# New stages between the layers of a three-layer graph attention kernel: residual products in the last edge stage, a bias in the table rows, self loop and share in one pass

## The chip, the cores and the metric

The kernel runs on one core of one Trainium2 chip. The metric is device microseconds (us) of one execution, lower is better. Three executions of the kernel before took 6745.49, 6760.7 and 6763.31 us, median 6760.7 us. In what follows PE is TensorE, DVE is VectorE, ACT is ScalarE, POOL is GpSimd and SP is SyncE.

## What is computed

There are 12500 nodes with 256 values each and 200000 directed edges, sorted by target. Two blocks follow each other, each with a residual and a layer norm. The first holds two graph attention layers of 4 heads, the second a linear map and one layer of 8 heads:

```python
def gat_conv(x, src, dst, W, att_src, att_dst, bias, n_nodes):      # layers 0 and 1, self loops appended to the edges
    h = (x @ W).reshape(n_nodes, Hh, Cc)
    alpha = leaky_relu((h * att_src).sum(-1)[src] + (h * att_dst).sum(-1)[dst])
    e = jnp.exp(alpha - segment_max(alpha, dst)[dst])
    w = e / jnp.clip(segment_sum(e, dst), 1e-16)[dst]
    return segment_sum(w[:, :, None] * h[src], dst).reshape(n_nodes, Hh * Cc) + bias

x = layernorm(x + gat_conv(relu(gat_conv(x, ...layer 0)), ...layer 1))
h = x @ W_lin + b_lin                                                # layer 2, without self loops, 8 heads of 32
x = layernorm(x + h + leaky_relu(gat(h @ W_gat, src, dst) + gat_bias, 0.01))
```

## The kernel before, in words

**Stages.** The nodes are 98 blocks of 128 (12500 padded to 12544), the edges 1568 tiles of 128 in 98 windows of 16 tiles, of which the last 5 tiles of the last window hold no edge. The program goes through `node_phase(None, 0)`, which builds the index tables, folds the weights and computes the table rows of layer 0, and then for each layer L through `edge_phase(L)`, `clear_semaphores()` and `node_phase(L, L + 1)` (`final_phase()` behind layer 2). Each of them is a block of its own: no engine enters the next before all have left the last. A table row holds a node's 256 products and its source terms for the heads, all in float32. I call the node stages before layer 1 and layer 2 the first and the second stage between layers.

**Edge stage.** For each window, POOL issues 16 indirect transfers (L1212), one for each tile, that gather the rows of the tile's source nodes into one of three row buffers. SP loads the window's index columns `loaded` (L1224), one-hot rows and masks. ACT turns the one-hot rows of the next window into a lookup matrix (L1248, L1251), copies the source terms out of the rows (L1262), clears the PSUM sums (L1242) and takes exponentials. PE turns the source terms (L1344), loads addresses into registers (L1194), turns the row sums (L1352), looks up the target terms (L1301), and then runs the products of the window before (L1287 for three extra tiles, L1294 for the 16 tiles) that add messages to the blocks' sums. DVE scans for the segment maximum (L1503), multiplies the rows by the weights (L1414), builds the one-hot matrices (L1406) and adds the finished sums to `acc`, which stays in SBUF for all 98 blocks with the sum of weights and the maximum of each head.

**Stages between layers.** DVE first works out two factors for every node and head at once, 392 columns (L689 to L711): the share by which the summed messages are divided, and the factor `own` of the self loop. SP loads the node's own table row from DRAM, one block at a time into three buffers (`n_looprow`), and before layer 2 also the input x (`n_resrow`). POOL multiplies the row by `own` (L657), and before layer 2 adds layer 1's bias and x (L665, twice). DVE adds this term to the shared-out sum (L772). The share itself is applied by DVE (L764) in the first of the two stages and by ACT (L549) in the second. Before layer 2 the layer norm follows on DVE (L781, L785, L789, L800; the root on ACT). PE turns the block (L891), ACT copies it back to SBUF (L565, L568), PE makes the products for the next table (L905, and L908 for the bias in three bfloat16 parts) and, before layer 2, the products with `w_lin` for the residual (L902, L903), to which DVE adds the node row (L807). ACT copies the table row (L576) and the target terms (L580, L581) and stores both from its own queue (L585, L589). At the end DVE splits the target terms of all blocks into three bfloat16 parts (L834, L836). The order on each engine is the order in which the loops emit, a fixed lag for each step behind the block's number.

**What clears the counters.** Between an edge stage and the node stage behind it POOL clears 71 semaphores one by one (L344 to L348), while the other engines stand at the block's border.

## Time and profile before

| | |
|---|---|
| three executions | 6745.49, 6760.7, 6763.31 us |
| the profiled execution | 6753.64 us, span 6751.8 us |
| granted TensorE clock, mean | 0.763 of full speed |
| busy share of the span | PE 72%, PE weight load 54%, DVE 75%, ACT 37%, POOL 72% |
| DMA | 995.73 MB, mean 147 GB/s over the span |
| gathers | 4704 instructions on L1212, 4488.4 us busy |

The span is that of one profiled execution. A busy share is a mean over stages that have different limits, so it does not say what bounds the kernel. Rows of the timeline show, in this order, the start in us from the span's start, the duration, the engine, the line, the operation, what is written and read, the shape and type, the count, and in square brackets how long the engine stood idle ahead of it and what ended that. "issue" means that nothing the profile shows was waited for.

### The profile page before, as it was taken

How to read it: one execution, taken by the hardware profiler on the slowest of the kernel's cores; microseconds unless marked ns; L12 is line 12 of the kernel's file. 1: busy time of each engine (PE TensorE's matmuls, PEld its weight loads, DVE VectorE, ACT ScalarE, POOL GpSimd, SP SyncE). 2: the span in 40 equal slices, each digit the busy share in tenths (PEclk: the TensorE clock that was granted, in tenths of full speed). 3: DMA queues.
4: the chain of work that ended last, by engine and by line, in shares of the span. 5: the costliest groups of instructions: out<-in, count | busy, mean ns of one | idle time of the engine just before them, and what ended most of it. 6: DMA issues, size and time to landing. Idle time of an engine off the chain costs nothing. (4 is left out here: it accounts for less than half of the span.)

```text
span 6751.8 us, 104146 instructions
## 1 busy us (share of the span) xinstructions
PE 4889.6 (72%) x21580; PEld 3649.8 (54%) x21581; DVE 5043.8 (75%) x15127; ACT 2499.9 (37%) x4364; POOL 4853.2 (72%) x5234
## 2 busy tenths in 40 slices
PE   6777777777776677777777777595777777777776
PEld 4555555555554555555555555474555555555553
DVE  5777777777777777777777777686777777777778
ACT  3333333333332633333333333393333333333335
POOL 2777777777774577777777777596777777777764
PEclk8777777777777877777777777797777777777777
DMA  8444444444443644454544544374555555555544
GB/s 273 141 140 143 140 140 144 140 140 144 140 141 95 176 144 143 141 145 141 145 141 141 145 141 145 102 232 144 145 149 145 147 148 145 149 145 145 149 132 153
DMA packets 476056, 995.73 MB, mean 147 GB/s; under 512 B 143982, under 2 KB 283556, under 8 KB 475522
## 3 DMA queue, kind: packets, MB, share of 16 engines
q0 software_dynamic: 226928, 635.50, 34.3%
q1 hardware_dynamic: 192448, 305.57, 14.2%
q10 hardware_dynamic: 56402, 51.96, 2.3%
q14 instruction: 227, 1.86, 0.1%
q8 instruction: 51, 0.84, 0.0%
HBM read 921.41 MB, written 71.22 MB: 147 GB/s over the span
## 5 line engine op out<-in xcount | busy, mean ns | idle before, releaser
L1212 POOL DMA_INDIRECT e_rows<-table,e_loaded x4704 | 4488.4, 954 | 1524.4 <-issue 1378.5
L1294 PE MATMUL e_p_mm<-e_rows,e_onehot 128*128 128x264 f32 x9408 | 2421.5, 414 | 0.0
L1294 PEld LDWEIGHTS e_p_mm<-e_rows,e_onehot 128*128 128x128 f32 x9408 | 1880.9, 206 | 348.8 <-issue 0.2
L1414 DVE TENSOR_TENSOR e_rows<-e_rows,e_p_e 128x1024 f32<-128x1024 f32 x1176 | 1418.7, 1206 | 0.0
L1406 DVE TENSOR_TENSOR e_onehot<-e_col,e_p_iota 128x512 f32<-128x512 f32 (+1 forms) x1470 | 951.0, 647 | 295.9 <-issue 293.9
L1503 DVE TENSOR_TENSOR_SCAN e_fwd<-e_mask,e_p_one 64x128 f32<-64x128 bf16 (+1 forms) x294 | 122.0, 415 | 1150.0 <-PE e_p_one L1344 1148.4
L1287 PE MATMUL e_p_mm<-e_xmsg,e_onehot 128*128 128x264 f32 x1764 | 875.4, 668 | 32.9 <-ACT e_p_mm L1242 17.7
L1270 ACT ACTIVATE e_rows<-e_gap 128x64 f32<-128x64 f32 (+1 forms) x294 | 80.5, 274 | 1969.9 <-DVE e_gap L1572 1969.9
L1301 PE MATMUL e_p_one<-ad_parts,e_onehotT 128*128 x5586 | 681.0, 192 | 119.8 <-issue 118.5
L1352 PE MATMUL e_p_small<-ident,e_fwd 64*1 64x64 f32 (+1 forms) x294 | 86.9, 295 | 864.3 <-issue 853.1
L1301 PEld LDWEIGHTS e_p_one<-ad_parts,e_onehotT 128*128 128x128 bf16 x5586 | 552.4, 106 | 291.5 <-issue 185.4
L1248 ACT ACTIVATE e_onehotT<-e_onehotT,minus_pidx 128x2432 bf16<-128x2432 bf16 x294 | 681.4, 2318 | 34.2 <-DMA e_pass<-pass_rows 33.9
L1251 ACT ACTIVATE e_onehotT<-e_onehotT,one_col 128x2432 bf16<-128x2432 bf16 x294 | 682.7, 2322 | 9.6
L1287 PEld LDWEIGHTS e_p_mm<-e_xmsg,e_onehot 128*128 128x128 f32 x1764 | 542.9, 328 | 169.3 <-issue 26.7
L1344 PE MATMUL e_p_one<-ident,e_srcc 128*64 128x128 f32 (+1 forms) x294 | 90.8, 309 | 644.1 <-ACT e_srcc L1262 643.8
L1352 PEld LDWEIGHTS e_p_small<-ident,e_fwd 64*1 64x1 f32 (+1 forms) x294 | 22.7, 77 | 918.5 <-issue 918.5
L1344 PEld LDWEIGHTS e_p_one<-ident,e_srcc 128*64 128x64 f32 (+1 forms) x294 | 36.8, 125 | 755.8 <-issue 755.8
L1392 DVE TENSOR_TENSOR acc<-acc,e_p_mm 128x264 f32 x1176 | 416.1, 412 | 28.8 <-PE e_p_mm L1294 28.8
L1262 ACT COPY e_srcc<-e_rows 128x64 f32<-128x64 f32 (+1 forms) x294 | 100.4, 342 | 800.1 <-DMA e_rows<-table,e_loaded 800.1
L1468 DVE TENSOR_TENSOR e_xmsg<-e_rows,e_p_e 128x256 f32 x882 | 358.7, 412 | 0.0
L1242 ACT COPY e_p_mm<-iota_d 128x1056 f32<-128x1056 f32 x294 | 303.2, 1031 | 29.9 <-DVEq L1455 29.9
L1275 ACT ACTIVATE e_factor<-e_p_small 128x4 f32<-128x4 f32 (+1 forms) x294 | 51.5, 175 | 618.0 <-PE e_p_small L1373 618.0
(238 smaller groups left out, 5626.5 us busy)
## 6 DMA issues: line engine op xcount, KB each, us to landing
e_onehotT<-rel_rows SPq DMA_DIRECT2D x294, 608.0 KB
e_rows<-table,e_loaded POOLq DMA_INDIRECT x4704
n_looprow<-table SPq DMA_DIRECT2D x196, 128.0 KB, 2.6
table<-n_row ACTq DMA_DIRECT2D x98, 132.0 KB, 1.9
table<-n_rows_out SPq DMA_DIRECT2D x14, 910.0 KB, 10.3
table<-n_row ACTq DMA_DIRECT2D x98, 130.0 KB, 3.0
n_inputs<-in_x_turned SPq DMA_DIRECT2D x14, 896.0 KB, 11.0
e_mask<-mask_rows SPq DMA_DIRECT2D x196, 64.0 KB
```

The lines of the kernel that those rows point to most:

```text
L1212: pool.indirect_dma_start(rows[k][:, g, 0:TW], None, table[L], bass.IndirectOffsetOnAxis(ap=idx[k][:, g:g + 1], axis=0)).then_inc(s_gat[k] ...
L1242: nc.scalar.copy(p_mm[:].rearrange("p (r n) -> p r n", n=BANK)[:, :, 0:MW], zero_col.unsqueeze(2).to_broadcast([P, REGIONS, MW])).then_inc ...
L1248: nc.scalar.activation(onehotT[k][:], onehotT[k][:], ACT.Square, bias=minus_pidx[:, 0:1]).then_inc(st["square"], 1)
L1251: nc.scalar.activation(onehotT[k][:], onehotT[k][:], ACT.Relu, bias=one_col[:, 0:1], scale=-1.0).then_inc(st["onehotT"], 1)
L1287: nc.tensor.matmul(p_mm[:, r:r + MW], onehot[:, G + e, :], xmsg[:, e, :], start=False, stop=True, skip_group_check=True)
L1294: ins = nc.tensor.matmul(p_mm[:, bass.ds(region, MW)], onehot[:, g, :], rows[k][:, g, :], start=False, stop=True, skip_group_check=True)
L1301: return nc.tensor.matmul(p_look[:, column], onehotT[k][:, slot * P:(slot + 1) * P], ad_parts[:, bass.ds(ad, 3 * H)], start=False, stop=Tr ...
L1344: nc.tensor.transpose(p_src[0:HG, 0:P], srcc[:].rearrange("p h g -> p (h g)"), ident[:]).then_inc(st["srcT"], 1)
L1392: last = nc.vector.tensor_tensor(sums, sums, p_mm[:, r * BANK:r * BANK + MW], ALU.add)
L1406: return nc.vector.tensor_tensor(onehot[:, slot:slot + n, :], col[k][:, column:column + n].unsqueeze(2).to_broadcast([P, n, P]), nodes.uns ...
L1414: return nc.vector.tensor_tensor(feats, feats, p_e[:, g4, :].unsqueeze(3).to_broadcast([P, 4, H, C]), ALU.mult)
L1468: nc.vector.tensor_tensor(xmsg[:, e, 0:D].rearrange("p (h c) -> p h c", h=H), feats, weight, ALU.mult)
```

## The change

The two node stages between layers become a function of their own, `between_phase`.

- **Residual.** The product of the normalised block with `w_lin`, its bias and the node row itself leave the second stage between layers. That stage stores the turned blocks to DRAM (`turned_dram`, two blocks to a transfer). In layer 2's edge stage each window takes one block: SP loads it (128 KB), PE multiplies it with `w_lin` plus the identity (L1379) and adds the bias from three bfloat16 parts (L1380), ACT copies the sum to SBUF (`summed`), SP stores it.
- **Bias of layer 1.** DVE adds it to the rows of layer 1's table in the first stage between layers, as it copies them out of PSUM (`biased_row`, L836). POOL's addition of the bias in the second stage goes. Since a node's weights sum to one, the sum is the same.
- **Self loop and share.** DVE computes `acc * share + term` with four instructions of 128x64 (L807), one for each head, in place of one pass for the share and one for the addition.
- **Factors.** `share` and `own` are worked out for the first 14 blocks, and for the other 84 in five pieces between the steps of the stream.
- **Normalisation** goes from DVE to ACT. Roots, reciprocals and shifts are taken over up to 7 blocks at once.
- **Transfers.** Own rows and x are loaded two blocks at a time, 8 blocks ahead. Table rows are stored by SP, 7 blocks (910 KB) at a time.
- **Borders.** `clear_semaphores` clears two ranges. The first three loads of `loaded` are issued at the end of the node stage. In every edge stage the last window has 11 tiles, not 16.

```diff
@@ tables of numbers
+LAST_TILES = -(-N_EDGES // P) - (WINDOWS - 1) * G
...
@@ clear_semaphores
-    for x in [*per_layer, *s.values(), *s_node, *s_loop, *s_res, *s_row, *s_out, *s_rst]:
-        pool.sem_clear(x)
+    for group in (per_layer, [*s.values(), *s_node, *s_loop, *s_res, *s_row, *s_out, *s_rst]):
+        first, last = group[0].num, group[-1].num
+        assert [x.num for x in group] == list(range(first, last + 1))
+        pool.sem_clear(range(first, last + 1))
...
@@ new: issued by SyncE at the end of each node stage
+    def first_columns(q):
+        for w in range(BUFS):
+            q.dma_start(loaded[w][:], col_dram[:, w * COL_W:(w + 1) * COL_W]).then_inc(s_idx[w], 16)
...
@@ between_phase(before) in place of node_phase(0, 1) and node_phase(1, 2)
+    N_PAIRS, N_TERM, N_VALUE, N_NODE, N_XT, N_ROWS, N_PT, N_PM = 4, 6, 22 if normed else 8, 6, 4, 2 if normed else 3, 3, 4
+    def load(j):
+        if j >= N_PAIRS:
+            sp.wait_ge(s["loop_term"], 2 * (j - N_PAIRS + 1))
+        pair = slice(2 * j * P, 2 * (j + 1) * P)
+        sp.dma_start(looprow[j % N_PAIRS][:], table[before][pair, 0:D].rearrange("(j p) n -> p j n", p=P)
+                     ).then_inc(s_loop[j % N_PAIRS], 16)
...
+    def store_turned(j):
+        sp.wait_ge(s["xT"], 2 * (j + 1))
+        sp.dma_start(turned_dram[2 * j:2 * (j + 1)].rearrange("j p e -> p j e"), xT[j % N_XT][:]
+                     ).then_inc(s_rst[j % N_XT], 16)
+    def store_rows(c):
+        sp.wait_ge(s["row"], (c + 1) * CHUNK)
+        sp.dma_start(table[after][c * CHUNK * P:(c + 1) * CHUNK * P, :].rearrange("(j p) n -> p j n", p=P),
+                     rows_out[c % N_ROWS][:, :, 0:D + HA]).then_inc(s_row[c % N_ROWS], 16)
...
@@ GpSimd, per block
-    ins = nc.gpsimd.tensor_tensor(heads(term, b, HB), heads(buf(looprow, b)[:], b, HB),
-                                  over(own3, b, HB), ALU.mult)
-    if normed:
-        for n, other in enumerate((bias_bc, buf(resrow, b))):
-            ins.then_inc(s["chain_p"], 1)
-            if n:
-                moved(pool, s_res, b)
-            pool.wait_ge(s["chain_p"], 2 * b + n + 1)
-            ins = nc.gpsimd.tensor_tensor(term, term, other[:], ALU.add)
-    ins.then_inc(s["loop_term"], 1)
+    if b == LEAD:
+        pool.wait_ge(s["prep"], 4)
+    ins = nc.gpsimd.tensor_tensor(out.rearrange("p (h c) -> p h c", h=HB), own_row,
+                                  both[:, 1, b, :].unsqueeze(2).to_broadcast([P, HB, C]), ALU.mult)
+    if normed:
+        ins.then_inc(s["part"], 1)
+        pool.wait_ge(s["part"], b + 1)
+        ins = nc.gpsimd.tensor_tensor(out, out, resrow[j % N_PAIRS][:, at, :], ALU.add)
+    ins.then_inc(s["loop_term"], 1)
...
@@ ScalarE
-    def share_out(b):
-        free(act, s["node"], b, value)
-        for h in range(HB):
-            c = slice(h * (D // HB), (h + 1) * (D // HB))
-            ins = nc.scalar.activation(buf(value, b)[:, c], acc3[:, b, c], ACT.Identity, scale=sh3[:, b, h:h + 1])
-        ins.then_inc(s["v1"], 1)
+    def normalise(b):
+        act.wait_ge(s["shift"], span_of[b] + 1)
+        free(act, s["turned"], b, N_NODE)
+        nc.scalar.activation(buf(node, b)[:], buf(value, b)[:], ACT.Identity, bias=shift[:, b:b + 1],
+                             scale=rinv[:, b:b + 1]).then_inc(s["node"], 1)
...
@@ VectorE
-    def value_share(b):
-        free(dve, s["node"] if normed else s["turned"], b, value)
-        num = acc[:, b * ACC_W:b * ACC_W + D]
-        nc.vector.tensor_tensor(heads(buf(value, b)[:], b, HB), heads(num, b, HB), over(sh3, b, HB), ALU.mult
-                                ).then_inc(s["v1"], 1)
-    def value_add(b):
-        v = buf(value, b)[:]
-        dve.wait_ge(s["v1"], b + 1)
-        if looped:
-            dve.wait_ge(s["loop_term"], b + 1)
-            nc.vector.tensor_tensor(v, v, buf(loopterm, b)[:], ALU.add).then_inc(s["value"], 1)
-    def normalise(b):
-        dve.wait_ge(s["rinv"], b + 1)
-        free(dve, s["turned"], b, node)
-        free(dve, s["resid"], b, node)
-        nc.vector.tensor_scalar(buf(node, b)[:], buf(value, b)[:], buf(mv, b)[:, 0:1], buf(rstd, b)[:, 1:2], ALU.subtract, ALU.mult
-                                ).then_inc(s["node"], 1)
-    def residual(b):
-        dve.wait_ge(s["mm"], b + 1)
-        if b >= len(resid):
-            moved(dve, s_rst, b - len(resid))
-        nc.vector.tensor_tensor(buf(resid, b)[:], buf(node, b)[:], buf(pr, b)[:, 0:D], ALU.add).then_inc(s["resid"], 1)
+    def value_sum(b):
+        if b == LEAD:
+            dve.wait_ge(s["prep"], 4)
+        dve.wait_ge(s["loop_term"], b + 1)
+        free(dve, s["node"] if normed else s["turned"], b, N_VALUE)
+        for h in range(HB):
+            cols = slice(h * C, (h + 1) * C)
+            last = nc.vector.scalar_tensor_tensor(buf(value, b)[:, cols], acc3[:, b, cols], both[:, 0, b, h:h + 1],
+                                                  buf(term, b)[:, cols], ALU.mult, ALU.add)
+        last.then_inc(s["value"], 1)
...
+    def biased_row(b):
+        c, j = divmod(b, CHUNK)
+        dve.wait_ge(s["mm"], b + 1)
+        if j == 0 and c >= N_ROWS:
+            landed(dve, s_row, N_ROWS, c - N_ROWS)
+            dve.wait_ge(s["att"], c - N_ROWS + 1)
+        nc.vector.tensor_tensor(rows_out[c % N_ROWS][:, j, :], buf(pm, b)[:, 0:WA], row_bias[:], ALU.add
+                                ).then_inc(s["row"], 1)
...
+    elif 0 <= i - 4 < BLOCKS:
+        biased_row(i - 4)
+    if i < BLOCKS:
+        value_sum(i)
+    if i == 1:
+        targets(late)
+    elif i == 3:
+        logits(late)
+    elif i == 5:
+        gaps(late)
+    elif i == 9:
+        totals(late, 2)
+    elif i == 11:
+        shares(late)
+    j, at = divmod(i - 17 if normed else i - 10, GROUP)
+    if at == GROUP - 1 and 0 <= j < BLOCKS // GROUP - 1:
+        dve.wait_ge(s["att"], (j + 1) * (GROUP // CHUNK))
+        split_terms(link, ad3, j, HA)
...
@@ TensorE, node stage
-        nc.tensor.matmul(buf(pr, b)[:, 0:D], buf(xT, b)[:, k, :], wlin[:, k, :], start=(k == 0), stop=False)
-    nc.tensor.matmul(buf(pr, b)[:, 0:D], sum_parts[:], bias_parts[:, 0:D], start=False, stop=True)
...
@@ edge_phase
+    def tiles_of(w):
+        return LAST_TILES if isinstance(w, int) and w == WINDOWS - 1 else G
...
+    for g in range(tiles_of(w)):
...
@@ edge_phase(2) alone (LINEAR)
+    def store_summed(b, done):
+        wait_apart(sp, st["kept"], done)
+        sp.dma_start(resid_dram[bass.ds(b * P, P), :], summed).then_inc(s_linout, 16)
+    def load_turned(b):
+        sp.dma_start(turned.rearrange("p k e -> p (k e)"), turned_dram[bass.ds(b, 1)].rearrange("o p e -> (o p) e")
+                     ).then_inc(s_turned, 16)
...
+    def add_linear(w, past):
+        wait_apart(pe, st["factor"], past)
+        wait_apart(pe, s_turned, count(pe, w * 16 + 16))
+        for c in range(2):
+            nc.tensor.matmul(p_small[:, LIN_AT:LIN_AT + D], turned[:, c, :], lin[:, c, :], start=c == 0, stop=False)
+        nc.tensor.matmul(p_small[:, LIN_AT:LIN_AT + D], one_parts, lin_parts, start=False, stop=True
+                         ).then_inc(st["linear"], 1)
...
+    nc.scalar.copy(summed, p_small[:, LIN_AT:LIN_AT + D]).then_inc(st["kept"], 1)
...
+    wait_apart(pe, *((st["kept"], now) if LINEAR else (st["factor"], past)))
-                    wait_apart(pe, st["factor"], past)
```

**The order, second stage between layers.** On POOL, from the last gathers of layer 1 on; `n_resrow` is the block's x. Before:

```order
L1212 DMA e_rows<-table,e_loaded 128x260 x32
L1125 UNCONDITIONAL_BRANCH
L345 UNCONDITIONAL_BRANCH
L348 ISA x71
L344 UNCONDITIONAL_BRANCH
L645 UNCONDITIONAL_BRANCH
L657 TENSOR_TENSOR n_loopterm<-n_looprow,n_own 128x256
L665 TENSOR_TENSOR n_loopterm<-n_loopterm,n_bias_bc 128x256
L665 TENSOR_TENSOR n_loopterm<-n_loopterm,n_resrow 128x256
```

In the changed kernel, from the border on:

```order
L1120 UNCONDITIONAL_BRANCH
L353 UNCONDITIONAL_BRANCH
L358 ISA x2
L352 UNCONDITIONAL_BRANCH
L666 UNCONDITIONAL_BRANCH
L680 TENSOR_TENSOR n_term<-n_looprow,n_both 128x256
L685 TENSOR_TENSOR n_term<-n_term,n_resrow 128x256
```

Each block has two instructions of 128x256 where it had three, and two clears stand where 71 stood.

On DVE in the same stage, one block of the steady part. Before (`n_pr` is the residual product in PSUM):

```order
L807 TENSOR_TENSOR n_resid<-n_node,n_pr 128x256
L800 TENSOR_SCALAR n_node<-n_value,n_mv,n_rstd 128x256
L789 RECIPROCAL n_rstd<-n_rstd 128x1
L785 BN_AGGR n_mv<-n_stats 128x2
L781 BN_STATS n_stats<-n_value 128x6
L772 TENSOR_TENSOR n_value<-n_value,n_loopterm 128x256
```

In the changed kernel, steps 9 to 11 of the stream, with the late factors (128x336) between the blocks:

```order
L817 BN_AGGR n_mv<-n_stats 128x2
L813 BN_STATS n_stats<-n_value 128x6
L807 SCALAR_TENSOR_TENSOR n_value<-acc,n_both,n_term 128x64 x4
L822 RECIPROCAL n_rinv<-n_root 128x3
L817 BN_AGGR n_mv<-n_stats 128x2
L813 BN_STATS n_stats<-n_value 128x6
L807 SCALAR_TENSOR_TENSOR n_value<-acc,n_both,n_term 128x64 x4
L795 RECIPROCAL n_limit<-n_limit 128x336
L796 TENSOR_TENSOR n_both<-n_both,n_limit 128x336
L797 TENSOR_TENSOR n_both<-n_both,n_limit 128x336
```

Three passes of 128x256 (L807, L800, L772) become four of 128x64, and the reciprocal serves several blocks.

**The order, layer 2's edge stage.** On PE, the start of a window. Before:

```order
L1344 MATMUL e_p_one<-ident,e_srcc 128x128
L1194 TENSOR_LOAD off_row x3
L1352 MATMUL e_p_small<-ident,e_fwd 1x128
L1352 MATMUL e_p_small<-ident,e_bwd 1x128
L1301 ISA
```

In the changed kernel (`e_lin` is `w_lin` plus the identity, and `as` is the tile that holds the turned block and the bias parts):

```order
L1397 MATMUL e_p_one<-ident,e_srcc 128x128
L1379 MATMUL e_p_small<-e_lin,as 128x256 x2
L1380 MATMUL e_p_small<-as 128x256
L1202 TENSOR_LOAD off_row x3
L1407 MATMUL e_p_small<-ident,e_fwd 1x128
L1407 MATMUL e_p_small<-ident,e_bwd 1x128
L1341 ISA
```

The linear product stands behind the turn of the source terms and ahead of the loads of the registers and of the turns of the row sums, which now also wait until ACT has copied the product out of `p_small`.

## Rows read from the trace of the kernel before

**Rows 1.** Costliest groups, gathers: busy, mean ns, then idle before them

```profile
L1212 POOL DMA_INDIRECT e_rows<-table,e_loaded x4704 | 4488.4, 954 | 1524.4 <-issue 1378.5
```

**Rows 2.** Timeline of POOL, borders of the three edge stages

```profile
130.96 1.04 POOL L1212 DMA_INDIRECT e_rows<-table,e_loaded  x1 [49.18 <-DMA e_loaded<-edge_cols]
...
2108.33 0.94 POOL L1212 DMA_INDIRECT e_rows<-table,e_loaded  x1 [0.30 <-issue]
...
2309.98 0.98 POOL L1212 DMA_INDIRECT e_rows<-table,e_loaded  x1 [12.67 <-DMA e_loaded<-edge_cols]
...
4277.99 0.94 POOL L1212 DMA_INDIRECT e_rows<-table,e_loaded  x1 [0.30 <-issue]
...
4595.20 0.97 POOL L1212 DMA_INDIRECT e_rows<-table,e_loaded  x1 [30.36 <-DMA e_loaded<-edge_cols]
...
6567.59 0.95 POOL L1212 DMA_INDIRECT e_rows<-table,e_loaded  x1 [0.30 <-issue]
```

**Rows 3.** Timeline, starts of the two stages between layers

```profile
2157.01 0.57 DVE L689 TENSOR_TENSOR n_ad<-ad_parts 128x392 f32<-128x392 bf16 x1 [5.15 <-PEq L344]
...
2171.89 0.84 POOL L657 TENSOR_TENSOR n_loopterm<-n_looprow,n_own 128x256 f32<-128x256 f32 x1 [62.62 <-DVE n_own L711]
...
4339.98 0.61 POOL L657 TENSOR_TENSOR n_loopterm<-n_looprow,n_own 128x256 f32<-128x256 f32 x1 [61.05 <-DVE n_own L711]
```

**Rows 4.** Timeline of PE, end of layer 0's edge stage

```profile
2142.25 8.13 PE L1294 MATMUL e_p_mm<-e_rows,e_onehot 128*128 128x264 f32 x32
```

**Rows 5.** Timeline of DVE, border into layer 1's edge stage

```profile
2307.35 0.11 DVE L1581 MEMSET e_inb<- 1x64 f32 x1 [0.57 <-PEq L359]
```

**Rows 6.** Timeline, first stage between layers, steady part

```profile
2230.63 0.38 PE L891 MATMUL n_pt<-ident,n_value 128*128 128x128 f32 x2
...
2231.74 0.38 PE L891 MATMUL n_pt<-ident,n_value 128*128 128x128 f32 x2
...
2234.34 1.18 POOL L657 TENSOR_TENSOR n_loopterm<-n_looprow,n_own 128x256 f32<-128x256 f32 x2 [2.29 <-DMA n_looprow<-table]
```

**Rows 7.** Timeline, second stage between layers, steady part; last row its end

```profile
4441.66 1.03 PE L902 MATMUL n_pr<-n_wlin,n_xT 128*128 128x256 f32 x4
...
4441.92 0.61 POOL L657 TENSOR_TENSOR n_loopterm<-n_looprow,n_own 128x256 f32<-128x256 f32 x1
...
4441.98 0.70 DVE L800 TENSOR_SCALAR n_node<-n_value,n_mv,n_rstd 128x256 f32<-128x256 f32 x1
...
4442.61 0.73 POOL L665 TENSOR_TENSOR n_loopterm<-n_loopterm,n_bias_bc 128x256 f32<-128x256 f32 x1
...
4442.64 1.08 PE L905 MATMUL n_pm<-n_wall,n_xT 128*128 128x272 f32 x4
...
4443.07 0.56 DVE L772 TENSOR_TENSOR n_value<-n_value,n_loopterm 128x256 f32<-128x256 f32 x1
...
4564.94 0.42 DVE L772 TENSOR_TENSOR n_value<-n_value,n_loopterm 128x256 f32<-128x256 f32 x1 [0.36 <-POOL n_loopterm L665]
```

**Rows 8.** Windows: length, busy PE, PEld, DVE, ACT, POOL, clock, DMA share, GB/s

```profile
4400.00:4500.00 100.00, 99.92 (x534) 79.58 (x533) 83.91 (x267) 91.43 (x399) 90.03 (x131) 1.00 0.77 234
```

**Rows 9.** DMA packets of 116 to 119 us, in the input stage

```profile
DMA packets 874, 0.89 MB, mean 297 GB/s; under 512 B 16, under 2 KB 874, under 8 KB 874
```

**Rows 10.** Timeline, one window of layer 2's edge stage

```profile
5505.72 0.30 PE L1344 MATMUL e_p_one<-ident,e_srcc 128*128 128x128 f32 x1 [2.20 <-ACT e_srcc L1262]
...
5508.99 0.37 PE L1352 MATMUL e_p_small<-ident,e_fwd 128*1 128x128 f32 x1 [2.96 <-issue]
...
5512.71 2.98 PE L1287 MATMUL e_p_mm<-e_xmsg,e_onehot 128*128 128x264 f32 x6
...
5521.86 0.18 ACT L1275 ACTIVATE e_factor<-e_p_small 128x8 f32<-128x8 f32 x1 [1.32 <-PE e_p_small L1373]
```

**Rows 11.** Timeline of DVE, operations of 128x64 back to back

```profile
2125.28 0.20 DVE L1561 SCALAR_TENSOR_TENSOR e_l<-e_l 128x64 f32<-128x64 f32 x1
2125.42 0.21 DVE L1563 SCALAR_TENSOR_TENSOR e_l<-e_l 128x64 f32<-128x64 f32 x1
```

906 lines of the change are left out of this document (461 added, 445 removed).

## The prediction

> **What bounds the kernel now.** I read the costliest groups first, because they show which engine is never let go. The gathers lead [rows 1]: 4704 of 0.95 us, and of the 1524 us that POOL idled ahead of them 1378 are "issue", that is, it waited for nothing. Then the timeline of POOL at the borders [rows 2]. The first gather starts at 130.96 us and the last at 2108.33, so the 1568 gathers of layer 0 come every 1.26 us; 4277.99 - 2309.98 and 6567.59 - 4595.20 give the same pace. The edge stages go by POOL's issue, about 20.2 us a window, and inside them nothing else can win time unless it gets slower than that. What remains is outside: 131.0 us ahead of the first gather, 201.7 us between 2108.33 and 2309.98, 317.2 us between 4277.99 and 4595.20, and 184.2 us behind 6567.59, of a span of 6751.8. Third come the two gaps themselves. The last gather is followed by the last products, which end at 2150.4 [rows 4]; a border with the clears; the factors; and the stream of 98 blocks, whose first term starts at 2171.89 and 4339.98 [rows 3]. POOL's last term ends 12.67 and 30.36 us before the next gather [rows 2], at 2297.3 and 4564.8, so the streams take 125.4 and 224.9 us, 1.28 and 2.29 us a block.
>
> **The change part by part**, against the profiled execution (6753.6 us, 7 below the median of the three runs).
>
> *Last window.* It issues 5 gathers less, 5 x 1.26 = 6.3 us, and the last products, 32 passes in 8.13 us [rows 4], fall to 22, which is 2.5 us less. Both stand on the path: 8.8 us, in three layers 26.4 us.
>
> *Clears.* At the border with the 71 clears DVE stood 5.15 us [rows 3]; at the one without them 0.57 us [rows 5], and a border with clears is two blocks, so 2 x 0.57. That leaves 4.0 us for 71, some 0.06 each; two cost 0.1. Three times 3.9 is 11.7 us.
>
> *Factors first.* From the first factor at 2157.01 to the first term at 2171.89 are 14.9 us [rows 3]. With 56 columns in place of 392 the same chain of some 15 small operations costs its fixed part: two dependent operations of 128x64 follow each other every 0.14 us [rows 11], with handshakes to ACT and POOL I take 4 us. The bounds are 2 (nothing but pitch) and 8. Gain 10.9 us in either stage, 21.5 with a small loss. The 84 late blocks cost DVE the rest, some 10 us, between blocks: nothing where DVE has room, which I come to.
>
> *First stage between layers.* PE turns a block every 2231.74 - 2230.63 = 1.11 us when fed [rows 6], but the stream ran at 1.28: POOL stood up to 2.29 us for an own row that had not landed [rows 6], with three buffers of one block. Eight blocks of lead remove that. Then PE at 1.13 gives 111 us. Against this DVE has now four operations of 0.14 (0.56) and the row with its bias, an addition of 128x264 like the 0.42 of L772 [rows 7], together 0.98, and it also has the late factors and the splits. I take 1.2 us a block, 118 us, and leave the drain of 12.67 as it is: the splits go into the stream, but the last store is 910 KB. 138.1 from first term to first gather becomes 130: 8 us won. Bounds: 0 and 20.
>
> *Second stage between layers*, the largest term. PE is busy 99.92 of 100 us at full clock there, and POOL 90 [rows 8]. PE's block holds the residual product, 0.98 us from L902 to L905 [rows 7]; without it 2.25 - 0.98 = 1.27 remain. ACT loses the share of four instructions and gains the normalisation, one of them. On POOL 0.61 + 0.73 remain of 0.61 + 2 x 0.73, that is 1.42 with a gap [rows 7]. The 534 matmuls of rows 8 are 12 a block, so a block took 2.25 us there, and DMA moved 234 GB/s x 2.25 = 527 KB in it at a share of 0.77 [rows 8]. The changed stage loads an own row and x and stores a table row and a turned block: the same 528 KB. Where the engines were full with packets of about 1 KB they moved 347 to 361 GB/s [rows 9], so 1.51 us a block. By the share of rows 8, 234 / 0.77 = 304 GB/s, it would be 1.74. DVE has 0.56, the statistics, which read one 128x256 as L772 does (0.42 at most), and some 0.2 of small ones, 1.2, but it shares something with POOL: L800 takes 0.70 beside L657, and L772 takes 0.56 beside POOL but 0.42 where POOL is done [rows 7]. The two engines' passes that stretch each other sum to 0.61 + 0.73 + 4 x 0.14 = 1.90 if they fully exclude each other, and the stretch in the rows is about a third of the overlap. I take 1.6 us a block, between 1.51 and 1.90. 98 x 1.6 = 157, with 8 us for the late factors and the splits, which now lie on an engine without much room. The drain was 30.4 us here and 12.7 in the first stage [rows 2]. The new one has spans of up to 7 blocks and a last store of 910 KB, but no splits of 392 columns: I take 23. That is 188 in place of 4595.20 - 4339.98 = 255.2 [rows 2, 3], 67 us won. Bounds: 151 + 13 = 164 (91 won) and 186 + 8 + 35 = 229 (26 won).
>
> The Trainium skill bears on this stage ("SBUF — State Buffer", section "Who interferes with whom"): VectorE with two inputs from SBUF contends with GpSimd for a lock that shuts the other out fully. The trace agrees only in part, with 0.56 and 0.70 in place of 0.42, far from the full 0.61 of a POOL pass on top. By the rule the stage goes at the sum of 1.90 us a block, which is a rival below.
>
> *Residual product in layer 2's edge stage.* 98 windows get, on PE, four float32 passes and a bfloat16 one, 0.98 us by the same work in rows 7; on ACT a copy of 128x256, about 0.4 us like the 0.42 of L1262 [rows 10]; on SP a load and a store of 128 KB. PE stands 2.96 us between L1344 and L1352 for its register loads and the scans [rows 10], and 2.20 us ahead of L1344. The product lies in front of the register loads, so it delays them by 1 us. What is queued behind the new wait for ACT's copy are the row sums, the lookups, the extras and the products, and these free the row buffer for which POOL waits. ACT's copy stands before the lookup matrix and the clear, so those come up to 2.6 us later. POOL is three windows ahead and issues every 20.2 us; ACT still stands 1.32 us late in the window [rows 10]. I take the window's chain as shorter than POOL's by 2 us, and the product as hidden: +0.5 us for the last window. Below nothing it can't be worth, as it takes nothing off POOL. If the cover is gone, each us of excess costs 97 us.
>
> *Preloads* of `loaded`: 0.6 us won in each stage, in the drain above, and 0.4 us at the first gather.
>
> **Sum.** -26.4 - 11.7 - 21.5 - 8 - 67 - 0.4 + 0.5 = -134.5; 6753.6 - 134.5 = 6619. As the profiled run lay 7 us below the median, I add 3 and forecast 6622 us.
>
> **The rivals.**
>
> A. *The second stage goes at the pace of DMA or POOL*, 1.42 to 1.51 us a block, and the drain is near the 12.7 of the first. 6619 - 98 x 0.13 - 7 = 6600. For it: POOL 0.61 and 0.73 were read while contended. Against it: DVE gets late factors besides.
>
> B. *DVE and POOL exclude each other*: 1.90 in place of 1.6, 98 x 0.3 = 29 us, 6648. For it speaks the stretch of L800 by 0.29; against it that L772 loses only 0.14. The same number comes out if DMA gives 304 GB/s (+14) and the drain stays at 30.4 (+7), 6640.
>
> C. *Layer 2's window gets a little longer than POOL's*: 0.6 us of excess x 97 = +58, 6677. Half of rows 10's chain runs at the low clock (the extras take 2.98 us for six passes at 0.50 each, where the products take 8.13/32 = 0.25 each [rows 4]), and what is moved later moves with it.
>
> D. *Slower than before.* The same chain exceeds POOL's by more than 134 / 97 = 1.4 us a window. The path is the source terms, the linear product (1.0, or 2.0 if the clock is still at half), the register loads (2.96) behind it, ACT's copy (0.4 and two handshakes), then lookup, clear and extras, each pushed back. With 3.9 us more against 2 of slack it costs 1.9 x 97 = 184: 6803. For it: PE is told to wait in order, and the register loads no longer lie beside the scans alone. Against it: PE stands 5.2 us in rows 10 at just this place.
>
> E. *The change gives half of it*: loads of two blocks don't feed POOL sooner, and the first stage wins nothing and the second only 26. 6619 + 8 + 41 = 6668.
>
> **How the numbers follow.** The forecast has a chance of 0.54 (its own range 6607 to 6637), A 0.15, B 0.12, C 0.07, E 0.06, D 0.04, and 0.02 for C in a size at which nothing changes on the whole. The range reaches over A and B and to E: 6588 to 6670. A change of 0.3%, 20 us, is about what a measurement of this kernel tells from none, since the three runs lie 18 us apart. Faster by more than that: forecast, A, B, C and E, 0.94. Within: 0.02. Slower: 0.04.
>
> **What would show it.** In the profile after: the last gather of each layer 6 us earlier; DVE's idle time at the border about 1 us, and POOL's first term 4 us behind DVE's first factor; a granted pace of L680 of 1.6 us in the second stage with DVE or POOL busy over 90% and PE below 85%; L807 of 128x64 at 0.2 each with a pitch of 0.14, or longer if B holds; gathers of layer 2 every 1.26 us still, with "issue" ahead of nearly all of them. Wrong it is if the gathers of layer 2 wait for PE's products in most windows, if POOL waits for own rows in the second stage, or if DVE is busy all of the stage with passes stretched beyond a third.

## The result and the profile after

The changed kernel takes 6719.15 us (median of 4 runs, 6703.58 to 6724.24), the kernel before 6762.01 in the same comparison: a ratio of 0.9936, 95% interval 0.9921 to 0.9951. I had forecast 6622 and a range that ended at 6670. The direction was right, but two thirds of the gain did not come. The profiled execution took 6703.6 us with a span of 6701.8, 50.0 less than before, and the borders show where it lies. The first rows are POOL's timeline after, at the places of [rows 2]:

```profile
132.43 1.04 POOL L1220 DMA_INDIRECT e_rows<-table,loaded  x1 [49.15 <-POOLq L382]
...
2093.25 0.95 POOL L1220 DMA_INDIRECT e_rows<-table,loaded  x1 [0.30 <-issue]
...
2139.59 1.18 POOL L680 TENSOR_TENSOR n_term<-n_looprow,n_both 128x256 f32<-128x256 f32 x2 [45.40 <-DVE n_both L797]
...
2305.20 0.99 POOL L1220 DMA_INDIRECT e_rows<-table,loaded  x1 [16.24 <-POOLq L577]
...
4264.29 0.94 POOL L1220 DMA_INDIRECT e_rows<-table,loaded  x1 [0.30 <-issue]
...
4310.65 0.61 POOL L680 TENSOR_TENSOR n_term<-n_looprow,n_both 128x256 f32<-128x256 f32 x1 [45.41 <-DMA n_resrow<-in_x_pad]
...
4536.87 0.97 POOL L1220 DMA_INDIRECT e_rows<-table,loaded  x1 [30.13 <-POOLq L577]
...
6520.76 1.03 POOL L1220 DMA_INDIRECT e_rows<-table,loaded  x1 [0.30 <-issue]
```

Differences of these starts, beside those of [rows 2, 3], give the whole account (a term is POOL's first operation of a block; all in us):

| stretch | before | after | change | forecast |
|---|---|---|---|---|
| start to first gather | 131.0 | 132.4 | +1.5 | -0.4 |
| layer 0, first to last gather | 1977.4 | 1960.8 | -16.6 | -6.3 |
| to the first term | 63.6 | 46.3 | -17.2 | -17.3 |
| first stage, term to gather | 138.1 | 165.6 | +27.5 | -8 |
| layer 1, first to last gather | 1968.0 | 1959.1 | -8.9 | -6.3 |
| to the first term | 62.0 | 46.4 | -15.6 | -17.3 |
| second stage, term to gather | 255.2 | 226.2 | -29.0 | -67 |
| layer 2, first to last gather | 1972.4 | 1983.9 | +11.5 | -5.8 |
| last gather to the end | 184.2 | 181.0 | -3.2 | -6.4 |

Three rows miss to the bad side: the first stage by 35 us, the second by 38, layer 2 by 17. Layer 0 came out 10 us better than forecast. The window rows of the changed kernel show the engines in the two node stages (length, then busy PE, PEld, DVE, ACT, POOL, clock, DMA share, GB/s, as in [rows 8]):

```profile
2180.00:2280.00 100.00, 88.36 (x401) 56.70 (x399) 99.14 (x359) 44.01 (x154) 40.78 (x67) 1.00 0.58 179
4350.00:4470.00 120.00, 86.79 (x402) 64.47 (x400) 119.31 (x397) 65.73 (x185) 85.50 (x124) 0.89 0.85 264
```

DVE is busy 99.1 of 100 us in the first stage and 119.3 of 120 in the second. In [rows 8] PE was the full one. The timeline of the first stage shows what a block costs DVE:

```profile
2229.63 0.43 DVE L836 TENSOR_TENSOR n_rows_out<-n_pm,n_row_bias 128x264 f32<-128x264 f32 x1
2229.98 0.86 DVE L807 SCALAR_TENSOR_TENSOR n_value<-acc,n_both,n_term 128x64 f32<-128x64 f32 x4
...
2231.11 1.16 DVE L807 SCALAR_TENSOR_TENSOR n_value<-acc,n_both,n_term 128x64 f32<-128x64 f32 x4
```

POOL beside it:

```profile
2230.99 0.61 POOL L680 TENSOR_TENSOR n_term<-n_looprow,n_both 128x256 f32<-128x256 f32 x1 [2.25 <-DVE n_value L807]
```

And PE:

```profile
2230.90 0.44 PE L893 MATMUL n_pt<-ident,n_value 128*128 128x128 f32 x2 [1.46 <-DVE n_value L807]
```

The four operations of L807 start at 2229.98 and the next pass at 2230.76, so they hold DVE for 0.78 us, not the 0.56 of the forecast. The next four, beside a pass of POOL, last 1.16 us where these last 0.86. PE, which was to set the pace, waits for them. From 2185 to 2255 us DVE did 185 of these operations, 46 blocks, and 6 us of splits, so a block took 1.385 us. The second stage looks the same; in its window row DVE did 60 blocks and 9 us of splits, 1.85 us a block. DVE's timeline there:

```profile
4400.94 0.39 DVE L813 BATCH_NORM_STATS2 n_stats<-n_value 128x6 f32<-128x256 f32 x1
4401.25 1.44 DVE L807 SCALAR_TENSOR_TENSOR n_value<-acc,n_both,n_term 128x64 f32<-128x64 f32 x4
4402.61 0.17 DVE L817 BATCH_NORM_AGGREGATE n_mv<-n_stats 128x2 f32<-128x6 f32 x1
```

POOL's at the same time:

```profile
4400.93 0.61 POOL L680 TENSOR_TENSOR n_term<-n_looprow,n_both 128x256 f32<-128x256 f32 x1 [0.36 <-DVE n_value L807]
4401.62 0.79 POOL L685 TENSOR_TENSOR n_term<-n_term,n_resrow 128x256 f32<-128x256 f32 x1
```

Here the four of L807 hold DVE from 4401.25 to 4402.61, 1.36 us, which is 0.58 over their own 0.78. POOL's two passes lie beside them for 1.08 us.

In layer 2, 14 of 1562 gathers start over 0.6 us late where before none did. This is the window ahead of one of them, first ACT:

```profile
5148.81 0.42 ACT L1294 COPY e_srcc<-e_rows 128x128 f32<-128x128 f32 x1 [1.17 <-DMA e_rows<-table,loaded]
...
5151.27 0.37 ACT L1301 COPY as<-e_p_small 128x256 f32<-128x256 f32 x1 [1.90 <-PE e_p_small L1380]
...
5156.12 1.03 ACT L1274 COPY e_p_mm<-iota_d 128x1056 f32<-128x1056 f32 x1
```

PE in the same window:

```profile
5149.53 0.30 PE L1397 MATMUL e_p_one<-ident,e_srcc 128*128 128x128 f32 x1 [0.51 <-ACT e_srcc L1294]
...
5153.28 0.37 PE L1407 MATMUL e_p_small<-ident,e_fwd 128*1 128x128 f32 x1 [2.12 <-issue]
...
5157.45 2.98 PE L1326 MATMUL e_p_mm<-e_xmsg,e_onehot 128*128 128x264 f32 x6 [0.85 <-ACT e_p_mm L1274]
```

And POOL's late gather at its end, for which the profile names no releaser:

```profile
5167.01 0.94 POOL L1220 DMA_INDIRECT e_rows<-table,loaded  x1 [1.78 <-issue]
```

PE's extras start 7.92 us behind the turn of the source terms (5157.45 - 5149.53), where [rows 10] have 6.99, and they now wait for ACT's clear of the sums (L1274). ACT in turn stood 1.90 us for the linear product and then had 4.6 us of lookup matrix ahead of the clear (5151.54 to 5156.12). The window shown is a usual one: from 4700 to 6400 us the extras wait for the clear 81 times (us in total, times, longest), where the kernel before has no such wait in the same stretch:

```profile
PE e_p_mm L1326 <- ACT e_p_mm L1274: 69.4, 81, 1.9
```

### The profile page after: what moved, and what is told of

The parts are those of the page before. It is cut to its first block and busy times, and to the rows that moved or that the text cites. A ratio compares the mean times of both kernels' runs of the same rounds, so it can differ in the third digit from the quotient of the medians.

```text
span 6701.8 us, 103647 instructions
## 1 busy us (share of the span) xinstructions
PE 4962.7 (74%) x21550; PEld 3674.2 (55%) x21551; DVE 5094.5 (76%) x15570; ACT 2401.8 (36%) x3644; POOL 4753.2 (71%) x5120
## 5 line engine op out<-in xcount | busy, mean ns | idle before, releaser
L1220 POOL DMA_INDIRECT e_rows<-table,loaded x4689 | 4459.8, 951 | 1542.5 <-issue 1379.8
L1326 PE MATMUL e_p_mm<-e_xmsg,e_onehot 128*128 128x264 f32 x1764 | 875.6, 669 | 112.8 <-ACT e_p_mm L1274 98.6
L1326 PEld LDWEIGHTS e_p_mm<-e_xmsg,e_onehot 128*128 128x128 f32 x1764 | 543.3, 328 | 251.6 <-issue 108.6
L1274 ACT COPY e_p_mm<-iota_d 128x1056 f32<-128x1056 f32 x294 | 303.2, 1031 | 29.5 <-DVEq L1513 29.5
```

The costliest lines, as they stand in the source:

```text
L1220: pool.indirect_dma_start(rows[k][:, g, 0:TW], None, table[L], bass.IndirectOffsetOnAxis(ap=idx[k][:, g:g + 1], axis=0)).then_inc(s_gat[k] ...
L1274: nc.scalar.copy(p_mm[:].rearrange("p (r n) -> p r n", n=BANK)[:, :, 0:MW], zero_col.unsqueeze(2).to_broadcast([P, REGIONS, MW])).then_inc ...
L1326: nc.tensor.matmul(p_mm[:, r:r + MW], onehot[:, G + e, :], xmsg[:, e, :], start=False, stop=True, skip_group_check=True)
```

## The experiments

Four groups of four, each group timed against the kernel before on one chip. A ratio is to the kernel before; the changed kernel has 0.9936. Stage times are differences of POOL's starts, as in the table above. In kernels that leave a stretch alone they repeat within 2 us for a node stage, 4 us from the last gather to the first term and 5 us for the gathers of a layer; c3 and c4 are an exception in layer 2 (below).

**a1, no linear product.**

```diff
-        LINEAR = L == 2
+        LINEAR = False
```

The final stage reads x in place of the residual, so the output lacks it.

> The changed kernel without the linear product in layer 2's edge stage: no turned block is loaded, multiplied, copied or stored, and the final stage reads x in place of the residual (same bytes). Theory 1: the product makes a window's chain so long that POOL waits for a free row buffer in about 15 windows; without it layer 2's gathers take 1964 to 1968 us from first to last in place of 1983.9, and the time falls by 16 to 20 us against the changed kernel, to about 6701. Theory 2: layer 2's gathers are slower for another reason (its larger rows and their traffic), and the time stays within 4 us of 6719.

Ratio 0.9907 (0.989 to 0.9923). Layer 2's gathers take 1963.4 us, 20.5 less than with the product, and none starts late; everything else stays. Theory 1 holds: the linear product costs 20 us, not 0.5.

**a2, the product and its copy ahead of the wait for the rows.**

```diff
+                    if LINEAR: add_linear(w, past)            # PE, ahead of the wait for "compact"
                     wait_apart(pe, st["compact"], now)
+                    nc.scalar.copy(summed, ...)               # ACT, ahead of the wait for the gathers
                     act.wait_ge(s_gat[k], gathered(w, turns))
```

> The changed kernel with the linear product and ACT's copy of it ahead of the wait for the window's gathered rows, not behind it. PE stood 0.5 to 2.9 us there. Theory 1 (the product costs because it stands in the chain from the gathered rows to the products of the window before): the 1.9 us leave that chain, layer 2's gathers take about 1966 us, time 6701 to 6705. Theory 2 (it costs PE and ACT time wherever it stands): no change within 4 us, 6719.

Ratio 0.996 (0.9946 to 0.9974): worse. Layer 2's gathers take 1997.2 us. Both theories are wrong here. ACT's copy of the source terms now stood behind the copy of the product, and with it behind the last products of the window before:

```profile
5150.90 1.03 PE L1379 MATMUL e_p_small<-e_lin,as 128*128 128x256 f32 x4
5151.76 0.27 PE L1380 MATMUL e_p_small<-as 65*128 65x256 bf16 x1
5153.13 0.30 PE L1399 MATMUL e_p_one<-ident,e_srcc 128*128 128x128 f32 x1 [1.10 <-ACT e_srcc L1299]
```

**a3, first stage: rows copied by ACT, without the bias of layer 1.**

```diff
-                    elif 0 <= i - 4 < BLOCKS:
-                        biased_row(i - 4)                     # DVE
+                    table_row(b - 3)                          # ACT, also in the first stage
```

> The changed kernel with the first stage's table rows copied out of PSUM by ACT, without layer 1's bias, so DVE has only its four operations L807 there. Theory 1 (L807 and POOL's pass exclude each other, and the row's addition only lay beside POOL's pass): a block takes 0.78 + 0.61 = 1.39 us as before, the stage from first term to first gather stays within 5 us of 165.6, time about 6716. Theory 2 (DVE is full with 0.78 + 0.35 and is only stretched a little by POOL): a block falls to PE's 1.11 to 1.13, the stage by 25 us to 140, time about 6694.

Ratio 0.9915 (0.9898 to 0.9931). The first stage takes 142.2 us in place of 165.6, as theory 2 had it, and still 4 us more than the 138.1 of the kernel before. But where DVE does nothing but L807 its row of the timeline shows the loss to POOL too:

```profile
2199.59 12.59 DVE L807 SCALAR_TENSOR_TENSOR n_value<-acc,n_both,n_term 128x64 f32<-128x64 f32 x45
```

45 operations in 12.59 us are 1.12 us for four; the whole run of 56 from 2198.41 on, 16.04 us, gives 1.15, and 0.78 is their own time. A pass of POOL (mean 0.66 from 2185 to 2255 us) so takes up to 0.37 from them, 0.56 of its length. That is neither full exclusion (theory 1) nor nothing.

**a4, no multiplication by `own` on POOL.** The output lacks the factor of the self loop.

```diff
-                    ins = nc.gpsimd.tensor_tensor(out..., own_row, both[:, 1, b, :]..., ALU.mult)
+                    # first stage: a copy of 8 columns, and L807 reads looprow; second stage: looprow + resrow
```

> The changed kernel without POOL's multiplication of the own row by its factor. In the first stage POOL only copies 8 columns, and L807 reads the loaded row; in the second stage POOL has one pass, own row plus x. Theory 1 (L807 and POOL's passes exclude each other): L807 of 128x64 takes about 0.2 us each in the first stage, a block 0.78 + 0.35 = 1.13 us, the stage falls by 24 us; in the second stage the only pass left lies partly beside the statistics, a block takes 1.5 us (where DMA's 528 KB also are), 98 x 0.35 = 34 us less. Time 6719 - 58 = 6661. Theory 2 (L807 takes what it takes without POOL): 6719 within 5 us.

Ratio 0.9847 (0.9831 to 0.9864). The first stage takes 138.2 us (-27.4), the second 191.9 (-34.3), as theory 1 had it: 58 expected, 62 found. The groups of the first stage show L807 (here line 805) at its own length:

```profile
L805 DVE SCALAR_TENSOR_TENSOR n_value<-acc,n_both,n_looprow 128x64 f32<-128x64 f32 x392 | 84.8, 279 | 2.7 <-DMA n_row_bias<-in_bias 2.7
```

In the second stage DVE is still full, and DMA is next with a share of 0.98:

```profile
4320.00:4440.00 120.00, 98.31 (x492) 73.91 (x490) 119.14 (x487) 82.14 (x231) 53.53 (x74) 0.94 0.98 319
```

**b1, the clear of the sums ahead of the copy.** This group ran on another chip, on which the kernel before takes 9459 us; its node stages agree with the others, its edge stages don't (below).

```diff
+                        if not first: clear_sums(past)        # ACT, layer 2
                         nc.scalar.copy(summed, ...)
                         lookup_rows(...)
-                    if not first: clear_sums(past)
```

> The changed kernel with ACT's order in layer 2's edge stage changed: the clear of the PSUM sums stands ahead of the copy of the linear product, not behind that copy and the lookup matrix. Nothing else moves, PE has the order of the changed kernel. Theory 1 (what makes a window longer is that the copy waits 1.9 us for PE and so holds back the clear, for which the three extra products then wait 0.85 us): those 0.9 us go, layer 2's gathers take 1965 to 1970 us in place of 1983.9, about 15 us faster than the changed kernel. Theory 2 (the length comes from PE's own 1.2 us, or from the register loads behind it): no change within 4 us.

Ratio 1.0165 (1.0148 to 1.0182). In all layers the windows take 29 us there, and POOL waits for PE. Part of it is in PE's rows behind the register loads, the waits of the weight loads of the turned row sums, in this run (us in total, times, longest):

```profile
PEld e_p_small L1409 <- issue: 2390.8, 294, 18.1
```

The same row of the changed kernel:

```profile
PEld e_p_small L1407 <- issue: 833.0, 294, 6.1
```

That is 8.1 us a window in place of 2.8. It is not all: other waits of the weight loads that have no releaser are longer here too, 911.6 us in place of 135.5 ahead of the turn of `e_seg` (L1425, in the changed kernel L1423) and 372.1 in place of 108.6 ahead of the extras (L1328, L1326). Why a chip does that no run shows. The theories of this run could not be told apart here; c1 repeats it. With the window's chain as the bound, layer 2's gathers took 3079.9 us here, 3181.2 in b2, which has the order of the changed kernel, and 2896.7 in b3, which has no linear product there. So here the linear product costs some 180 to 280 us (b3 also issues the last window's five extra gathers), which is my rival D, and the order is worth 1.03 us a window.

**b2, value in two passes.**

```diff
-                    for h in range(HB): scalar_tensor_tensor(... 128x64 ...)
+                    link(nc.vector.tensor_tensor(v..., acc3..., share..., ALU.mult))
+                    nc.vector.tensor_tensor(v, v, buf(term, b)[:], ALU.add)
```

> The changed kernel with value = acc x share + term as two passes of 128x256 (0.35 us each without POOL) in place of four of 128x64 (0.195 each, 0.78). Theory 1 (DVE is the bound in both stages, and the one pass saves no DVE time, since its four pieces cost more than two whole passes): about 0.08 us a block less, 8 us less in either stage, less what their two-input reads lose more to POOL; 5 to 16 us faster than the changed kernel. Theory 2 (the one pass is the cheaper form as there is one handshake and one reading of the value less): slower by 10 us or more.

Ratio 1.0233 (1.0216 to 1.025) on that chip. The first stage takes 169.5 us (b1: 165.0), the second 222.8 (226.3): together 1 us. Neither theory holds; over both stages four pieces and two passes cost DVE the same.

**b3, the kernel before without its residual products.** The residual lacks the products.

```diff
-    for k in range(2): nc.tensor.matmul(buf(pr, b)[:, 0:D], buf(xT, b)[:, k, :], wlin[:, k, :], ...)
```

> The kernel before without the two float32 residual products in its second stage (the residual is then the node row and the bias alone). PE, at 2.25 us a block, was the bound. Theory 1: it falls to 1.27, but ACT was busy 91 of 100 us (2.06 a block) and POOL 90 (2.07), so the stage goes at 2.1 to 2.15: 10 to 15 us of 255 won. Theory 2: the stage goes at PE's or DMA's pace, 1.5 to 1.6, 60 us or more won.

Ratio 0.9997 (0.9988 to 1.0007). The second stage takes 248.8 us, 6 less than [rows 2, 3] give. All 6 lie behind the stream: from the first term to the end of the last one it takes 226.4 us, in the kernel before 224.9. So the 0.98 us a block that left PE won nothing there, and neither theory's gain came. POOL does as many operations in 100 us as in [rows 8], 131, and waits for nothing:

```profile
6180.00:6280.00 100.00, 66.58 (x346) 45.63 (x347) 84.18 (x259) 89.91 (x391) 90.18 (x131) 1.00 0.78 230
```

ACT is as busy as POOL in this row; which of the two sets the pace, b5 tells.

**b5, the kernel before without the products and without the addition of the bias.**

```diff
-    for n, other in enumerate((bias_bc, buf(resrow, b))):
+    ins = nc.gpsimd.tensor_tensor(term, term, buf(resrow, b)[:], ALU.add)
```

> The kernel before with both left out, the residual products and POOL's addition of layer 1's bias in the second stage. Theory 1: ACT is next at 2.06 us a block (it still shares out the sums, copies four things and issues the stores), 15 to 20 us won. So the new stage needed its other moves too. Theory 2: these two are all that the new stage lives on, and 65 us or more are won.

Ratio 0.9951 (0.9934 to 0.9967). The second stage takes 206.4 us, 49 less, between the 15 to 20 of theory 1 and the 65 of theory 2, and 42 less than b3. As one pass of POOL makes these 42, it was POOL that set the pace in b3, at 2.3 us a block, and in the kernel before too, beside the full PE. Now ACT is the bound, as theory 1 said, but at 1.91 us a block and not at 2.06:

```profile
6150.00:6250.00 100.00, 80.28 (x417) 54.97 (x418) 96.39 (x313) 99.31 (x471) 70.25 (x105) 1.00 0.93 279
```

That is 20 us shorter than the changed kernel's new stage, which put the share back on DVE. The traffic is the same, as the old stage stores the residual where the new one stores the turned block. So with the product and the bias done elsewhere, as in the change, the old stage should beat the new one; no run has the two together.

**c1, b1's kernel on a chip like the first.**

> The same kernel as in the earlier run of this name (ACT clears the PSUM sums ahead of the copy of the linear product), again, since that run fell on a chip where the register loads of a window take some 5 us longer, so that in all three layers the window's chain and not POOL's issue set the pace. There the reordering won 101 us of layer 2's stage against the other order, 1.03 us a window. Theory 1, for a chip where the kernel before takes about 6750: layer 2's gathers take 1965 to 1970 us in place of 1983.9. Theory 2: no change within 4 us.

Ratio 0.9948 (0.9931 to 0.9964), layer 2's gathers 1986.3 us: no gain. The wait had moved. ACT now stands for DVE's reading of the sums, and PE for the copy behind it, as ACT's timeline shows:

```profile
5159.87 1.04 ACT L1274 COPY e_p_mm<-iota_d 128x1056 f32<-128x1056 f32 x1 [4.02 <-DVEq L1515]
5160.84 0.37 ACT L1303 COPY as<-e_p_small 128x256 f32<-128x256 f32 x1
```

PE in that window:

```profile
5161.35 0.37 PE L1409 MATMUL e_p_small<-ident,e_fwd 128*1 128x128 f32 x1 [3.55 <-ACT as L1303]
```

**c2, shorter spans at the end of the second stage.**

```diff
-    spans += [(BLOCKS - 7, 3), (BLOCKS - 4, 2), (BLOCKS - 2, 1), (BLOCKS - 1, 1)]
+    spans += [(77, 4), (81, 4), (85, 3), (88, 3), (91, 2), (93, 2), (95, 1), (96, 1), (97, 1)]
```

> The changed kernel with shorter spans of roots, reciprocals and shifts for the last 21 blocks of the second stage (4, 4, 3, 3, 2, 2, 1, 1, 1 in place of 7, 7, 3, 2, 1, 1). POOL's last term ended 30 us before the next gather, where I had forecast 23. Theory 1: ACT and PE are 10 to 14 blocks behind DVE at its end, because a span of 7 is handed on only when its last block has its mean; shorter spans take 3 to 5 blocks of 1.26 us off the drain, 4 to 6 us, less 1 for the additional small operations. Theory 2: the drain is ACT's and PE's own work of the whole stage, and nothing changes.

Ratio 0.9938 (0.9921 to 0.9954). The second stage takes 221.7 us, 4.5 less, and POOL's wait ahead of the next gather is 25.6 in place of 30.1. Theory 1 holds for the stage. The whole time shows nothing of it; layer 2's gathers took 3.8 us more in this trace.

**c3, c1's and c2's edits together, and the first stage's rows copied by ACT with layer 1's bias added on PE.**

```diff
+    table_row(b - 3)                                          # ACT, first stage
+    last = nc.tensor.matmul(out, sum_parts[:], bias_parts[:], start=False, stop=True)
```

> The changed kernel with three edits: the clear ahead of the copy, the short spans, and in the first stage the rows copied by ACT and layer 1's bias added by PE as a bfloat16 product of three parts (0.12 us a block), so DVE keeps L807 alone. Theory 1: layer 2 -15 us, drain -4, first stage: DVE 0.78 + 0.37 lost to POOL = 1.155 (as the run without the bias showed), PE 1.11 + 0.12 = 1.23 sets the pace, 98 x 0.155 = 15 less, +2 for splitting the bias. Together 32 us faster than the changed kernel, ratio to before about 0.989. Theory 2: the gains overlap or PE's longer block costs what DVE gains in the first stage; then half of it, 0.991.

Ratio 0.9919 (0.9902 to 0.9935). The first stage takes 145.7 us, 20 less; PE is busy 99.3 of 100 us in it. In the node stages theory 1 holds. But layer 2's gathers take 1997.4 us, 11 more than in c1, which has the same edge stage, and in c4 1998.9. What makes them longer no run shows.

**c4, two of the four heads of the self loop on ACT.**

```diff
+    for h in range(HB // 2, HB):                              # ACT, second stage
+        nc.scalar.activation(buf(term, b)[:, cols], looprow..., ACT.Identity, scale=both[:, 1, b, h:h + 1])
```

> The kernel with those three edits and a fourth: in the second stage ACT multiplies two of the four heads of the own row by their factor, POOL the other two and the addition of x. POOL's passes fall from 1.39 to some 1.1 us a block, ACT's work rises from about 1.05 to 1.5. Theory 1 (the second stage goes at DVE's 1.25 us plus 0.43 of each us in which POOL works): DVE's block falls from 1.85 to about 1.7, 15 us off the second stage. Theory 2: ACT, which is emitted in one order, delays the normalisation and the stage gets no faster or up to 10 us slower.

Ratio 0.9894 (0.9877 to 0.991). The second stage takes 203.8 us, 18 less than c3. Theory 1 holds. It is now some 3 us shorter than b5's old stage.

**d1, copy, clear, lookup matrix.**

```diff
                         nc.scalar.copy(summed, ...)
+                        if not first: clear_sums(past)
                         lookup_rows(...)
-                    if not first: clear_sums(past)
```

> The changed kernel with ACT's order in layer 2's edge stage: copy of the linear product, then the clear of the PSUM sums, then the lookup matrix of the next window (the changed kernel has the clear last). With the clear ahead of the copy, ACT stood 3.8 us for DVE's reading of the sums, and PE 3.4 us for the copy: the wait had only moved. Theory 1 (the extras wait 0.85 us for the clear, as ACT waits 2.1 us for the product and then has 4.7 us of lookup matrix ahead of it): in this order the clear is done some 3 us earlier, the lookup matrix is not needed before the next window, and layer 2's gathers take 1965 to 1972 us in place of 1983.9, 12 to 18 us won. Theory 2 (it is PE's 1.3 us): within 4 us of the changed kernel.

Ratio 0.991 (0.9893 to 0.9927), layer 2's gathers 1967.9 us, 16 less: theory 1 holds. ACT's clear comes before the lookup matrix and the extras no longer wait for it:

```profile
5151.41 1.04 ACT L1274 COPY e_p_mm<-iota_d 128x1056 f32<-128x1056 f32 x1 [0.32 <-DVEq L1515]
```

PE's extras in that window, right behind the row before:

```profile
5154.80 0.24 PE L1420 MATMUL e_p_small<-ident,e_outb 1*128 1x1 f32 x1
5155.00 2.98 PE L1328 MATMUL e_p_mm<-e_xmsg,e_onehot 128*128 128x264 f32 x6
```

**d2, the passes on PE alone**, without copy and stores (no residual in the output).

```diff
-                        nc.scalar.copy(summed, p_small[:, LIN_AT:LIN_AT + D]).then_inc(st["kept"], 1)
```

> The changed kernel with the linear product on PE and its loads, but without ACT's copy and the stores (the final stage reads x in place of the residual). Theory 1 (ACT's wait and copy, with all that stands behind them, make the windows long): layer 2's gathers take 1964 to 1968 us, as in the run without the product. Theory 2 (PE's own 1.3 us do): 1980 to 1985, as in the changed kernel.

Ratio 0.9909 (0.9892 to 0.9926), layer 2's gathers 1966.9 us.

**d3, copy, loads and stores alone**, without the passes (the residual is the loaded block).

```diff
-                    for c in range(2): nc.tensor.matmul(p_small[:, LIN_AT:LIN_AT + D], ...)
+                    pe.sem_inc(st["linear"], 1)
```

> The changed kernel without the linear product's five passes on PE, but with ACT's copy (of the loaded block), PE's wait for it, the loads and the stores. Theory 1 (ACT waits 2.1 us for the product, which is most of the harm, and nothing waits here): 1964 to 1970 us for layer 2's gathers. Theory 3 (it is neither engine but the loads and stores of 128 KB a window and SP's order behind them): 1980 to 1985.

Ratio 0.9915 (0.9899 to 0.9932), layer 2's gathers 1968.8 us. Theory 1 holds in both. Either half alone lies 3 to 5 us over a1's 1963.4, about as far as equal kernels lie apart, and d3 has the traffic too; together they cost 20.5. It is ACT's wait for the passes with the clear behind it that costs, and d1 wins 16 of the 20.5 by moving the clear alone.

**d4, d1 with the three edits of the node stages** (c2's, c3's and c4's).

> The clear between copy and lookup matrix, together with the three edits of the node stages (short spans; rows by ACT with the bias on PE; two heads of the self loop on ACT). With the clear ahead of the copy these gave 0.9894 of the kernel before and 1998.9 us in layer 2's gathers. Theory 1: layer 2's gathers take 1968 us, 30 us less, ratio 0.985. Theory 2 (the order of the clear does nothing): 1984 us, 0.987.

Ratio 0.9844 (0.9827 to 0.986), median 6641.27 us against 6749.73 of the kernel before: the best version, 0.9 points under the changed kernel. First stage 143.2, second 203.9, layer 2's gathers 1965.6: theory 1 holds. The first stage is still 5 us over the 138.1 of the kernel before. In the second stage DVE is still the bound, with ACT and DMA close behind:

```profile
4330.00:4450.00 120.00, 103.60 (x465) 68.11 (x466) 119.29 (x458) 107.98 (x356) 76.89 (x139) 0.96 0.93 298
```

## Why the prediction was wrong

*Last window, clears, factors: right.* From the last gather to the first term I gave 17.3 us less in either stage (2.5 + 3.9 + 10.9), and the trace has 17.2 and 15.6. The parts fit too: ahead of the first stage the last products take 5.31 us in place of 8.13, DVE stands 1.39 us at the border in place of 5.15, and the first term starts 3.84 us behind the first factor, where I had 4. That the second gain is 1.6 us smaller lies in the kernel before (62.0 against 63.6); after the change both stretches take the same (46.4 and 46.3). Layer 0's gathers take 10 us less than the five missing ones explain. One gather takes 957 ns in the mean there before and 951 after, which makes these 10 us over 1567 of them. 1959 to 1964 us is what all 12 later kernels on chips of that speed show, which have the 11 last tiles too, so the value after is steady; the 1977.4 of before rests on one trace, and why its gathers were longer stays open.

*First stage, the step "DVE has now four operations of 0.14 (0.56)", with the row "together 0.98", and "I take 1.2 us a block".* This term of the sum was mis-sized. The 0.14 came from [rows 11], an operation of the same shape with a constant factor; L807 takes its factor from a column and two inputs from different tiles, and it costs 0.195; which of these makes it longer no run shows. With the row's 0.35, DVE alone is at 1.13, as long as PE. On that comes what POOL takes from it, 0.25 where the pass partly lies beside L836, which reads PSUM and is not stretched (0.42 or 0.43 in all rows). 1.385 a block, 98 x 0.185 = 18 us over my 1.2. The 0.22 between my 0.98 and 1.2 was to hold the late factors (some 10 us from 2144.9 on) and six splits of some 1.6 us; now they come on top. With a first wait of 2.3 us for the bias and 16.2 us from POOL's last term to the next gather, where I had 12.67, they are the rest. a3 and a4 show it from both sides: either the row or POOL's pass away, and the stage falls by 23 or 27 us.

*Second stage, the step "I take 1.6 us a block".* Same cause, and again a term of the sum that was mis-sized. DVE's own work is 0.78 + 0.47 = 1.25, near my 1.2, and POOL's two passes add 0.60, which makes 1.85; 98 x 0.25 = 24 us. Rival B had 1.90 and came nearest: I gave it 0.12. That it came so near is luck. Its sum (0.61 + 0.73 + 0.56) has L807 too short; with the measured 0.78 full exclusion would give 2.12, and the stage took 1.85. The Trainium skill ("SBUF — State Buffer", section "Who interferes with whom") speaks of an exclusive lock on the ports that the two engines share. a3's 0.37 us lost for a pass of 0.66, and the 0.58 lost beside 1.08 us of passes in the second stage, are less than that: the rule as I read it, that both times add up whole, is not what these traces show. A bit over half of a pass was lost in both stages.

The drain, from POOL's last term to the next gather, was 30.1 us, not 23; c2 shows that the spans make 4.5 of these 7. The late factors and splits, for which I had 8 us, are the rest of the 38.

Two readings beside this sum were wrong as well. I took PE, full at 2.25 us a block, for what bound the old stage; b3 and b5 show that POOL held it at 2.3 us even without the product, and ACT stood next at 1.91. And I gave DMA a floor of 1.51 us from 347 to 361 GB/s, where [rows 9] have 297 in the mean; a4, with DMA at a share of 0.98, moved 319, which for 528 KB is 1.66 us. Of my own signs of being wrong the last one came true: DVE was busy all of the stage, and L807 was stretched from 0.78 to 1.36 us.

*Layer 2, the step "I take the window's chain as shorter than POOL's by 2 us, and the product as hidden".* The 2 us were right, the second half was not. It was rival C in a small size, 17 to 20 us in place of 0.5. ACT's wait for the gathers, the slack of the chain, shows how near it was, here from the waits of 4700 to 6400 us of the kernel before (us in total, times, longest):

```profile
ACT e_srcc L1262 <- DMA e_rows<-table,e_loaded: 183.8, 84, 3.2
```

Of the changed kernel:

```profile
ACT e_srcc L1294 <- DMA e_rows<-table,loaded: 101.0, 63, 4.4
```

And of d1:

```profile
ACT e_srcc L1294 <- DMA e_rows<-table,loaded: 173.1, 79, 4.0
```

2.2 us a window fell to 1.2, and since windows differ, some were over: 14 gathers came late. I had counted ACT's copy and PE's passes each against its own engine's room. What mattered was the order behind the copy on ACT, which I named ("those come up to 2.6 us later") and then costed at nothing. On the chip of group b, with the longer waits of PE, the same chain is the bound everywhere, and b2, which has the changed kernel's order, loses 2.3% against the kernel before: rival D at its full size.
